# When the adjacency groups of the first graph layer may be read, and where unwanted cells are written

## The reference, cut to what matters

```
src, dst   # 106250 edges each, sorted by dst; 50000 random pairs both ways + 6250 self loops
h = relu(layernorm(x))                                      # [6250, 128]
summed = segment_sum(h[src], dst, num_segments=6250)        # mean over neighbours
out = (summed / deg) @ Wl.T + bl + h @ Wr.T                 # SAGE layer 1, then normalised,
                                                            # batch norm, SAGE layer 2
x = x + out
# then an 8-relation layer (two hops), a sum-aggregating layer, an attention layer
```

## Time and profile before

| | |
|---|---|
| median of 3 runs | 5368.31 us (5365.86 to 5370.98) |
| the profiled execution | 5368.31 us, of which the span of instructions is 5366.5 us |
| TensorE busy | 3267.3 us (61%) |
| GpSimd busy | 3069.5 us (57%) |
| VectorE busy | 2026.5 us (38%) |
| first SAGE layer's dense products | about 332 to 1180 us of the span |
| scatter of the adjacency | about 40 to 1133 us |
| mean granted TensorE clock | 0.709 of full |

### The profile page before, as it was taken

How to read it: one execution, slowest core, us unless ns; L and a number is a source line. 1 busy time by engine, 2 the same in 40 slices (tenths; PEclk the granted TensorE clock), 3 DMA queues, 4 the chain that set the end, 5 groups by cost and what they waited for, 6 DMA issues and landing times. The chain is left out here.

```text
span 5366.5 us, 69161 instructions
## 1 busy us (share of the span) xinstructions
PE 3267.3 (61%) x19534; PEld 2183.4 (41%) x19535; DVE 2026.5 (38%) x6104; ACT 958.0 (18%) x2127; POOL 3069.5 (57%) x3180
## 2 busy tenths in 40 slices
PE   4357544558997555555554444444479955777777
PEld 2124322234444334334333333333334434666665
DVE  7441101033114322222222222222231157888886
ACT  0010000001003100000000000000010016888885
POOL 5777777730000577777776777777700006777773
PEclk8678767779998655555555555555589966888887
DMA  8521010113224422222222221222232202333322
GB/s 223 144 97 49 24 48 24 48 72 121 96 95 120 115 74 79 80 80 76 80 80 56 52 53 52 52 53 52 51 123 94 96 24 59 68 69 68 67 67 65
DMA packets 370426, 408.73 MB, mean 76 GB/s; under 512 B 89191, under 2 KB 305078, under 8 KB 360374
## 3 DMA queue, kind: packets, MB, share of 16 engines
q1 hardware_dynamic: 268854, 295.73, 17.2%
q0 software_dynamic: 101504, 112.13, 9.7%
HBM read 299.65 MB, written 107.98 MB: 76 GB/s over the span
## 5 line engine op out<-in xcount | busy, mean ns | idle before, releaser
L633 POOL DMA_INDIRECT GS<-xw_table,stage x1664 | 1571.9, 945 | 1182.7 <-issue 1109.9
L1120 PE MATMUL psum<-HA,HT 128*128 128x512 fp8e4 (+1 forms) x5733 | 1211.0, 373 | 458.3 <-DMA HA<-adj 411.6
L1072 PE MATMUL psum<-GS 128*128 128x96 f32 x3328 | 774.1, 409 | 1034.4 <-DMA GS<-xw_table,stage 1014.4
L1072 PEld LDWEIGHTS psum<-GS 128*128 128x128 f32 x3328 | 697.6, 310 | 1110.4 <-issue 1110.4
L633 POOL DMA_INDIRECT HA<-p_table,stage x676 | 652.2, 965 | 750.2 <-ACT stage L916 549.7
L667 POOL DMA_INDIRECT adj<-cell_value,cell_i x832 | 838.5, 1008 | 291.0 <-issue 249.1
L1120 PEld LDWEIGHTS psum<-HA,HT 128*128 128x128 bf16 x5733 | 549.7, 99 | 1093.7 <-issue 456.4
L1577 DVE TENSOR_TENSOR HA<-HA,psum 128x96 f32 x208 | 53.1, 255 | 1357.1 <-PE psum L1072 1357.1
L1563 DVE TENSOR_SCALAR GS<-iota,HT,wt 128x96 f32<-128x96 f32 x1680 | 434.9, 356 | 158.7 <-issue 157.7
L1831 DVE SCALAR_TENSOR_TENSOR GS<-psum,keep,O 128x512 f32<-128x512 f32 (+1 forms) x26 | 18.7, 720 | 1054.3 <-PE psum L1140 737.3
L731 ACT ACTIVATE stage<-cell_i 128x16 int32 (+1 forms) x104 | 22.2, 215 | 1264.9 <-PE psum L1072 1264.9
(11 more groups left out here) (340 smaller groups left out, 3619.0 us busy)
## 6 DMA issues: line engine op xcount, KB each, us to landing
HA<-adj SPq DMA_DIRECT2D x39, 1600.0 KB, 6.5
HA<-adj SPq DMA_DIRECT2D x39, 1536.0 KB, 9.8
HT<-dst_rows SPq DMA_DIRECT2D x212, 256.0 KB
xw_table<-HT SPq DMA_DIRECT2D x100, 512.0 KB, 3.2
adj<-O SPq DMA_DIRECT2D x13, 3136.0 KB, 27.2
GS<-xw_table,stage POOLq DMA_INDIRECT x1664, 2.5
adj<-cell_value,cell_i POOLq DMA_INDIRECT x832
HA<-p_table,stage POOLq DMA_INDIRECT x676
```

The costliest lines, as they stand in the source:

```text
L633: nc.gpsimd.indirect_dma_start(out=to, out_offset=None, in_=table, in_offset=bass.IndirectOffsetOnAxis(ap=idx, axis=0)).then_inc(done, 16)
L1072: last = nc.tensor.matmul(bank[h][:, 0:WINDOW], G3[g][:, j, :], S_pair[h][:, t, :], start=(t == 0), stop=(t == 2 * GT - 1))
L1120: last = nc.tensor.matmul(bank[s][:, 0:w], Hs4[:, b, t, :], adj_tile[s][:, b * GW:b * GW + w], start=(b == 0 and t == 0), stop=(b == SRCS ...
```

## The change

Three places change. The wait of line 520 gets other numbers: it was the whole part of (268 g + 347) / 16, at most 208, and is 17 g + 20, at most 208. For the 13 dense groups:

| dense group | 0 | 1 | 2 | 3 | 4 | 5 | 6 | 7 | 8 | 9 | 10 | 11 | 12 |
|---|---|---|---|---|---|---|---|---|---|---|---|---|---|
| before | 21 | 38 | 55 | 71 | 88 | 105 | 122 | 138 | 155 | 172 | 189 | 205 | 208 |
| now | 20 | 37 | 54 | 71 | 88 | 105 | 122 | 139 | 156 | 173 | 190 | 207 | 208 |

The bound of line 1930 follows it, by the same instruction with other constants. And the table `trash_i` counts the other way: place (partition p, column t) had byte 1024 p + t of the trash region and now has byte 128 t + p. So the 128 places of one tile, which lay 1024 bytes apart, now lie side by side.

```
@@ load_adjacency
-                        sp.wait_ge(landed, min(GROUPS, (67 * (4 * g + 3) + 131 + 15) // 16))
+                        sp.wait_ge(landed, min(GROUPS, 17 * g + 20))
@@ the tables of GpSimd
-            nc.gpsimd.iota(trash_i, [[1, COLS]], base=0, channel_multiplier=1 << 10,
+            nc.gpsimd.iota(trash_i, [[P, COLS]], base=0, channel_multiplier=1,
@@ needs_rest
-                ch(V.tensor_scalar(of_group, lo, 67 / 16, 131 / 16, ALU.mult, ALU.add))
+                ch(V.tensor_scalar(of_group, lo, 17 / 4, 7.25, ALU.mult, ALU.add))
```

## The result

The changed kernel takes 5396.42 us (5394.22 to 5399.05, 6 runs) against 5368.01 us: 28.4 us slower; the ratio is 1.0051 with a 95% interval of 1.0041 to 1.0061. I had forecast 5378.5 us with a range of 5373.5 to 5383.5. The direction was right, and the time lies outside that range, 18 us above the forecast.

A forecast was written before the change was run, and what follows sets the result against it. GpSimd's scatter was taken to bound this stage through `landed`, with group 11's count setting the layer's end. Terms 0 + 0 + 10.15 + 0 + 0 + 0 on 5368.31 gave 5378.5 us, range 5373.5 to 5383.5.

The forecast's parts named there:

- The waits: SyncE's loads of the dense groups in the first layer: new landing counts cost 10.15 us at group 11, 0 at all others.
- The term of 10.15 us for group 11: Its load waits for `landed` 207 instead of 205: two more landings at 5.07 us each, range 10.05 to 10.9.
- the other groups: Dense groups 0 to 10 and 12: changed or unchanged counts cost 0 at the end; group 12 has 30 us to spare.
- the start of TensorE: TensorE's first matmul on dense group 11 at about 1134.6, 6.83 us after its load starts, as before.
- the 45 us of idleness: TensorE's idle time ahead of dense group 11 grows from 40.13 us to 45.2.
- the even landings: `landed` 206 and 207 come at an even 5.1 us, 207 at 1127.75, since group 11's load has not left.
- The clock: TensorE's start on group 11 after longer idleness: same clock level as before, cost 0, with 1 us either side.
- The trash table: Unwanted bytes of the last scatter group, now side by side: cost 0, from -1.2 to 3.5 us, all on `landed` 208.
- my signs of being wrong: Group 11's load near 1117, TensorE waiting ahead of group 12, `landed` 208 later than 1145, or first sum near 1200.
- The rival of the trash queue: Neighbouring trash bytes written one after the other, 0.2 us each, make TensorE wait 19 us for group 12: about 5397; 5%.
- absorbed: Something else ends last between 1166 and the second SAGE layer, so group 11's delay costs nothing: 5368.3 or slightly under; 6%.
- The slow path: The bound in `needs_rest` fires and passes gather 832 tiles again, over 1 ms each: above 6400; below 1%.

## Why the prediction was wrong

- *The waits.* Right in each step. The term of 10.15 us for group 11 measured 10.3 alone, the other groups 0, the start of TensorE, the 45 us of idleness and the even landings as written.
- *The clock.* Right alone (group 11's first half took 18.89 us with the waits alone, 18.58 before). In the changed kernel the granted clock fell to 0.50 in the pause in the middle of group 11, and the second half took 1.65 us more. I had not priced a pause, since I had forecast none.
- *The trash table: the step that failed.* I wrote from -1.2 to 3.5 us, took 0, and said "all of it falls on `landed` 208, which has 30 us to spare". Both halves of it were wrong. The size: 35 us (37.6 - 2.2 with the trash table alone). The upper bound of 3.5 us was read from a landing that was crowded by a load, and no row of the trace had two byte writes beside one another; I took the nearest row as if it bounded something that it doesn't contain. The path: I looked for who waits for the landing, and not for which transfer is in flight beside the writes. With group 11's load released by 207, its 3.2 MB leave at 1130.25, and tiles 830 and 831 follow at 1131.8 and 1133.1. It is the number 207 of the same change that puts the load there, and TensorE waits 14.3 us for its second half. With the trash table alone, where group 11 starts two landings earlier and leaves less to spare, the same late landing does make TensorE wait for group 12. Of my signs of being wrong, "`landed` 208 later than 1145" is the one that came true.
- *The rival of the trash queue* had 5%, and its 5397 is close to the 5396.4 measured, but for the wrong reason. It had 0.2 us a byte (measured 0.144) and let TensorE wait ahead of group 12. With the 35 us measured that path gives next to nothing: `landed` 208 at 1170.0 and 7.6 us from there to TensorE's start, as with the trash table alone, make 1177.6. Without the pause of 14.5 us and the 1.65 us of clock TensorE would have come to group 12 at 1177.7 (1193.9 - 16.15). The 14.3 us were paid one load earlier. That the number fits is luck.
- *The Trainium skill* spoke against this edit: "DMA: Bandwidth & Descriptors", Specifications, that writes below 512 bytes become a read, a modification and a write. No run here shows these steps. A queue of neighbours, 35.4 us for 246 bytes, is what they could give. But the same rule holds for the kernel before, which lands in 2.2 us with 1024 bytes between the places, and for 64 bytes between them, where it is 2.2 us too. So the price is not that of a small write but that of small writes to one place, and the 512 of the rule is not the distance that matters here.
- *The other rivals.* The delay was not absorbed in any run at the usual pace; in the changed kernel the shift is 28.0 us at the first sum and 29.3 at the end of the span (5395.8 - 5366.5). On the longer-running chips the new waits with 64 bytes measured 1.0005 (0.9990 to 1.0019), where 10 us would be 1.0015: there it isn't settled. The slow path didn't fire: TensorE has the same 19534 matmuls.
- *A reading without effect.* The earlier trace rows shows TensorE's first nine slices between 3 and 7 and not at 4 or 5, and GpSimd idle for four slices and a part. No term of the sum hangs on it.

## What to carry to other kernels

A dump for unwanted elements is memory like any other: spread what one indirect DMA writes there, since places that lie only a few bytes apart queue on one another, and the queue holds up a load that is in flight behind it (here 64 bytes apart were enough). When a wait is moved, ask not only who is released later but what the released transfer will now be in flight with. And where an edit does something that no row of the trace contains, the nearest row is no bound; the doubt belongs in the range.

## What the runs showed of the hardware that I had not expected

- 246 single-byte writes side by side in HBM landed 35.4 us later than with 1024 bytes between the places of a tile, 0.144 us each as a mean. At 4 bytes apart the two tiles took 10.6 us more than at 64 apart, at 16 apart 0.9; at 64 apart it was the 2.2 us of 1024.
- From some 5 us behind such a scatter they held up a load that was in flight: 438 GB/s from 1134 to 1136 us, and 26 from 1138 to 1155. A load that was through by then was not touched.
- They stopped TensorE as well, at places where the code has no wait: 5.5 and 4.7 us at the usual pace, 6.4 to 16.9 us on the longer-running chips (where other stops at these lines last at most 3.3 us), each ending at the landing or at most 2.2 us ahead of it. The way by which they do it isn't shown.
- On two further chips the kernel before takes 6575 and 6578 us instead of 5368. In every trace from there TensorE stops for some 430 us in all between single matmuls of the first layer's loops, and GpSimd waits for it, up to 21 us at a time. There neither one landing less nor 64 bytes apart with the new waits could be told from no change, so what bounds a stage on one chip need not bound it on another.
